# A fused attention and expert kernel: the weight maxima and weight splits of the opening in another order

## The reference, cut to what matters

```python
x = L0_attn_x                                   # (4, 1024, 512) float32
xn = _layernorm(x, axis=-1)
x = x + attn(xn, Wq, bq, Wk, bk, Wv, bv, Wo, bo) + ffn(xn, gate_w, w1, w2)

# attn: 16 heads of 32
q, k, v = proj(Wq, bq), proj(Wk, bk), proj(Wv, bv)
scores = einsum('bhqd,bhkd->bhqk', q, k) / sqrt(D)
scores = where(causal, -inf, scores) + alibi_bias
out = einsum('bhqk,bhkd->bhqd', softmax(scores), v) @ Wo.T + bo

# ffn: 8 experts, every token goes to its 2 best
probs = softmax(x @ gate_w.T); topw, sel = top_k(probs, 2); topw /= sum(topw)
out = sum over the chosen e of topw[e] * ((silu(g_e) * u_e) @ w2[e].T)   # g_e, u_e = split(x @ w1[e].T)
```

## Time and profile before

| | us |
|---|---|
| median of 3 runs | 1640.9 |
| lowest and highest | 1637.94, 1645.32 |
| the profiled execution's own time | 1637.66 |
| its span, first to last instruction | 1635.9 |
| PE busy in the span | 1479.2 (90%) |
| mean granted TensorE clock | 0.976 |

### The profile page before, as it was taken

One profiled execution on the slowest core, in us unless ns is written; L12 is line 12 of the kernel. 1 busy time (PEld: TensorE's weight loads), 2 busy tenths in 40 slices (PEclk: granted clock), 3 DMA queues, 4 the chain that ended last, 5 costly groups with the idle time before them and its releaser, 6 DMA issues.

```text
span 1635.9 us, 35508 instructions
## 1 busy us (share of the span) xinstructions
PE 1479.2 (90%) x12763; PEld 889.9 (54%) x12763; DVE 1047.6 (64%) x2485; ACT 888.6 (54%) x2029; POOL 567.1 (35%) x595
## 2 busy tenths in 40 slices
PE   3799988998998899989799898999889999999995
PEld 1465555655555555655455466565356656566563
DVE  6688787666778767777878877777334333333331
ACT  4477776665777666676766565667312222222221
POOL 3111132121113222112311134231215777777775
PEclk9899999999999999999999899999989999999998
DMA  6244431433423243542324241324687888788783
GB/s 254 74 131 114 123 91 58 112 104 101 118 90 96 88 136 115 149 128 76 97 64 116 77 115 52 87 78 164 220 260 110 136 129 141 129 140 136 127 145 45
DMA packets 171350, 193.28 MB, mean 118 GB/s; under 512 B 87536, under 2 KB 121072, under 8 KB 171056
## 3 DMA queue, kind: packets, MB, share of 16 engines
q1 hardware_dynamic: 143760, 151.67, 34.3%
q0 software_dynamic: 26128, 37.24, 13.7%
q10 hardware_dynamic: 1296, 2.11, 0.3%
HBM read 93.45 MB, written 53.74 MB: 90 GB/s over the span
## 4 chain that ended last, share of the span: by engine, by line
PE 67%; DVE 11%; issue 7%; ACT 5%; DMA 4%; SPq 4%; POOL 2%; DVEq 0%; POOLq 0%; ACTq 0%
PE S L1175 15%; PE T L1098 11%; PE O L1114 7%; PE S L1055 5%; PE S L1087 5%; PE O L1206 4%; PE M L1206 4%; PE M L1055 4%; DVE arena L1480 4%; SPq L932 3%; PE S L1072 2%; PE M L1137 2%; PE M L1072 2%; ACT arena L1670 2%; DVE arena L1491 1%
## 5 line engine op out<-in xcount | busy, mean ns | idle before, releaser
L1480 DVE CUSTOM_DVE_ANT_0 arena<-S,cF,nsl 128x1024 f32<-128x1024 f32 (+7 forms) x512 | 413.2, 811 | 60.0 <-PE S L1087 56.9
L1098 PE MATMUL T<-cF,arena 128*128 128x128 f32 x2304 | 368.1, 281 | 77.4 <-ACT arena L1684 42.6
L1670 ACT ACTIVATE arena<-arena,mneg 128x1024 f32<-128x1024 f32 (+7 forms) x512 | 395.4, 772 | 47.8 <-DVE mneg L1480 46.8
L1684 ACT ACTIVATE arena<-T 128x512 f32<-128x512 f32 (+3 forms) x544 | 241.8, 457 | 276.3 <-PE T L1098 274.2
L1098 PEld LDWEIGHTS T<-cF,arena 128*128 128x128 f32 x2304 | 267.9, 142 | 179.2 <-ACT arena L1684 47.8
L1175 PE MATMUL S<-arena 128*128 x1704 | 270.4, 316 | 8.9 <-issue 8.9
L1823 POOL DMA_INDIRECT out<-arena x142 | 222.1, 1564 | 106.8 <-ACT arena L1730 53.7
L1491 DVE COPY arena<-T 128x512 f32<-128x512 f32 (+3 forms) x288 | 153.6, 536 | 138.8 <-PE T L1098 137.0
L1175 PEld LDWEIGHTS S<-arena 128*128 128x128 f16 x1704 | 167.9, 99 | 108.4 <-issue 10.3
L1114 PE MATMUL O<-arena 128*32 128x128 f32 (+1 forms) x3328 | 211.3, 330 | 8.3 <-DVE arena L1511 7.1
L1087 PE MATMUL S<-arena 96*128 96x512 f16 (+3 forms) x768 | 213.1, 332 | 3.8 <-DMA arena<-arena 2.5
(11 more groups left out here) (187 smaller groups left out, 1822.3 us busy)
## 6 DMA issues: line engine op xcount, KB each, us to landing
arena<-arena SPq DMA_DIRECT2D x192, 128.0 KB, 2.4
arena<-in_w1T SPq DMA_DIRECT2D x64, 352.0 KB, 3.5
arena<-in_x SPq DMA_DIRECT2D x64, 256.0 KB, 3.4
w_d<-arena SPq DMA_DIRECT2D x32, 352.0 KB, 2.9
arena<-w_d SPq DMA_DIRECT2D x16, 704.0 KB, 7.2
arena<-in_w2T SPq DMA_DIRECT2D x32, 256.0 KB, 2.9
out<-arena SPq DMA_DIRECT2D x32, 256.0 KB, 3.2
xn_d<-arena SPq DMA_DIRECT2D x24, 256.0 KB, 2.0
```

What stands on the lines that cost most here:

```text
L1098: tp = pe.transpose(z[:, (c - c0) * P:(c - c0 + 1) * P], ring[u % 4][:, c * P:(c + 1) * P], idf)
L1480: dve.tensor_tensor_reduce(ring[r][:, 0:w], SBK[o.bank["score", u]][:, 0:w], rel[:, S - w:S], nsl[:, hh:hh + 1], 3.0e38, ALU.add, ALU.min, ...
L1670: act.activation(ring[r][:, 0:w], ring[r][:, 0:w], ACT.Exp, bias=mneg[:, m:m + 1], scale=-1.0, accum_out=rs[:, k, c:c + 1]).then_inc(sems[ ...
L1684: act.activation(PT[k][:, h, to_:to_ + gap * (c1 - c0 - 1) + 1:gap, :], TB[o.bank["tr", u, i]][:, 0:n].rearrange("p (c n) -> p c n", n=P), ...
```

## The change

Both halves' statistics stay first. Then the first half is normalised as before, and its transposes go to the two T banks in place of the M banks. All four `tops` now come ahead of any `xn` of the second half; the second half's four `xn` stand in pairs around the two steps of `gmax` and `gtop`. The weights' group 0 is split into q, k and v (pieces 0, 1, 2, of 512 columns each), and pieces 3 to 6 are the other groups. PE's waits follow: q of group 0 waits for `wql` 0, k for 1, v for 2, anything later for 6. `scales` 1 is cut in three: 1 (seven small instructions), 3 (`cq`, `bq`, `bk`) and 4 (the gate's, the slopes and `rel`). The second half's turns are placed around the first `qk`. k of group 0 gets a float32 place of its own, in the second half of `raw`, so a `qk32` waits for the `qkl` two before it. The float16 halves of tiles 3 to 6 move from `st` to the arena behind `PT1`, so the waits for their release move from `qkh` to the first `pt` of unit 8 and up. `otop` moves ahead of `vsb`, and `woh` and `wol` are cut into halves.

```diff
     def ln_turn(b, half, i):
...
+        bank = "M" if b else "T"
...
-    for half in range(2):
-        for i in range(7):
-            if i > 2:
-                ln_turn(0, half, i - 3)
-                flush()
-            if i < 4:
-                ln_tile(0, half, i)
-        if half == 0:
-            add("tops", 0)
+    for i in range(7):
+        if i > 2:
+            ln_turn(0, 0, i - 3)
+            flush()
+        if i < 4:
+            ln_tile(0, 0, i)
     load["act"] = load["dve"]
-    for c in range(1, 4):
+    for c in range(4):
         add("tops", c)
...
     for part in range(2):
-        for _ in widest("w", part):
-            pass
+        first = widest("w", part)
+        next(first)
+        ln_tile(0, 1, 2 * part)
+        ln_tile(0, 1, 2 * part + 1)
+        next(first)
     add("scales", 0)
     add("wqh", 0)
+    add("scales", 1)
+    add("wqh", 1)
     add("wql", 0)
-    for c in range(4):
-        add("wqh", 1 + c)
-    add("scales", 1)
+    add("wql", 1)
+    add("scales", 3)
+    for i in range(2):
+        ln_turn(0, 1, i)
+        flush()
+    add("wqh", 2)
+    add("wqh", 3)
+    add("wql", 2)
     start = qkv_steps(0, 0)
     for i in range(16):
         next(start)
         flush()
-        if i == 5:
-            add("wql", 1)
+        if i == 2:
+            for t in (2, 3):
+                ln_turn(0, 1, t)
+            flush()
+            add("wqh", 4)
+        elif i == 4:
+            add("wql", 3)
+            add("wqh", 5)
+        elif i == 8:
+            add("scales", 4)
+            add("wqh", 6)
+        elif i == 11:
+            add("wql", 4)
+    next(start)
+    add("otop")
     for _ in start:
         flush()
-    for c in range(1, 4):
-        add("wql", 1 + c)
+    add("wql", 5)
+    flush()
+    add("wql", 6)
 
     def first_rest():
-        add("otop")
-        yield
...
-        add("woh")
-        yield
-        add("wol")
+        add("woh", 0)
+        yield
+        add("wol", 0)
+        add("woh", 1)
+        yield
+        add("wol", 1)
         yield
...
-        return w[:, :, :, 0:P] if part == 0 else w[:, part - 1, :, P:E]
+        return w[:, :, part, 0:P] if part < 3 else w[:, part - 3, :, P:E]
+
+    def t32_at(b, g, qk, half):
+
+        return raw[:, 1, 0:512] if b == g == 0 and qk else t32[:, 0, :]
...
-                if (b, g, qk, half) != (0, 0, 0, 0):
-                    n = 4 * (b * NG + g) + 2 * half + qk - 1
-                    on.wait_ge(sems["qkl"], n + 1)
+                n = 4 * (b * NG + g) + 2 * half + qk
+                if n > 3:
+                    on.wait_ge(sems["qkl"], n)
+                elif n > 1:
+                    on.wait_ge(sems["qkl"], n - 1)
```

More of the change, by code:

```diff
@@ L188, in ln_turn @@
         key = "xtp", b, half, i
-        take_m(*key)
+        bank = "M" if b else "T"
+        if b:
+            take_m(*key)
+        else:
+            o.take("T", *key)
         add(*key)
@@ L195, in rest @@
             o.count["xt", b, half, i] = o.count["xt", b, half, i, en]
-            o.leave("M", key, ("xt", b, half, i))
+            o.leave(bank, key, ("xt", b, half, i))
         later.append(rest)
@@ L1129, in tensor @@
                 if third == 0:
-                    on.wait_ge(*at("wol"))
+                    on.wait_ge(*at("wol", 1))
                     for g in range(NG):
@@ L1490, in vector @@
                     on.wait_ge(*at("pv", u // 8 * 8 - 9))
+                elif u >= 8:
+                    on.wait_ge(*at("wol", 1))
+                    for t in range(3, 7):
+                        on.wait_ge(*at("xtp", 0, t // 4, t % 4))
+                        on.wait_ge(*at("xnd", 0, t // 4, t % 4))
                 dve.tensor_copy(PT[k][:, h, to_:to_ + gap * (c1_ - c0_ - 1) + 1:gap, :],
@@ L1628, in scalar @@
                 tt = half * 4 + i
-                tz = MBK[o.bank["xtp", b, half, i]][:, :].bitcast(F16)
+                tz = (MBK if b else TB)[o.bank["xtp", b, half, i]][:, :].bitcast(F16)
                 on.wait_ge(*at("xtp", b, half, i))
@@ L1680, in scalar @@
                 else:
-                    on.wait_ge(*at("wql", 4))
+                    on.wait_ge(*at("wql", 6))
                     if u >= 8:
-                        on.wait_ge(*at("wol"))
+                        on.wait_ge(*at("wol", 1))
+                        for t in range(3, 7):
+                            on.wait_ge(*at("xtp", 0, t // 4, t % 4))
+                            on.wait_ge(*at("xnd", 0, t // 4, t % 4))
                 act.activation(PT[k][:, h, to_:to_ + gap * (c1 - c0 - 1) + 1:gap, :],
```

56 lines of the change are left out of this document (30 added, 26 removed).

## The result

The changed kernel takes **1629.88 us**, median of 5 runs (1626.0 to 1632.59); the kernel before took 1640.9, median of 5 (1637.94 to 1645.32; the three runs known ahead and two more). The ratio is 0.9928 with a 95% interval of 0.9902 to 0.9954: 11.0 us less. The profiled execution is one of the faster ones: own time 1626.15, span 1624.4, PE busy 1476.2 us (91%), mean granted clock 0.974.

A forecast was written before the change was run, and what follows sets the result against it. PE was taken as the bound from about 100 us on, so the opening's saving shifts everything behind it: 10.7 at unit 2 plus 0.5 from woh is 11.2, so 11; 1640.9 - 11 = 1629.9 us, range 1625 to 1637.

The forecast's parts named there:

- The maxima and the xn: Opening on DVE: three further reductions follow the first at once in 5.06; second half's first two xn take 0.48 each.
- The chain ahead of the copy: Opening: PE's turn of tile 3, gmax, two small DVE steps and two xn, then the copy of the maxima to 25.05.
- Waits behind POOL: DVE beside POOL's second-half xnl: 0.6 of waiting for the scale and 0.6 for the first wql, bounds 0 and 1.16 each.
- Rival 1: Small DVE scale instructions wait for POOL's xnl; gain falls by 2.7 to 8.5, time 1632.4; chance 0.24.
- q's low clock: First q matmuls on PE: q takes 3.94 as before, start to start, its first matmuls at 1.2 GHz.
- The second float32 place: k of group 0's own float32 place: worth nothing by itself, since PE still has v to do.
- The first mx: End of the opening on DVE: at 52.5, behind two wql of 1.36, against 59.3; 6.8 earlier.
- otop: Its 2.28 moves to a DVE pause before v; it and PE's wait for it are gone behind the first mx.
- The halves of woh and wol: Output weights' split: about 1 us of PE's 2.68 wait can return; taken as 0.5, bounds 0 and 1.9.
- The pt assignment: Different choice of ACT or DVE for some pt between units 0 and 16: 0, bounds -0.5 and 0.5.
- Nothing of the change reaches there: From about 100 us on PE is the bound, so what the opening saves shifts everything behind it.
- Rival 3: Long part of the kernel: mean granted clock falls to 0.96, costing 24 us, time 1654; chance 0.04.

The follow-up runs named there:

- tops_late: Changed kernel with only the first reduction of the weights ahead of the second half's xn, the other three behind them; 1631.48 us, ratio to before 0.9932.
- pt_before: Changed kernel with the fifteen pt copies of units 0 to 14 that differ put back on the engines of the kernel before; 1623.39 us.
- again: The changed kernel's same code profiled once more, for a second trace; 1624.93 us.
- warm: Changed kernel plus 27 idle matmuls with overwritten results in PE's pauses of the opening; 1620.77 us, ratio to before 0.9879.
- t32_one: Changed kernel with q and k of group 0 sharing one float32 place again, as before; 1623.02 us.
- otop_late: Changed kernel with otop, the maximum of the output weights, behind the first mx again, as before; 1634.85 us.
- o_whole: Changed kernel with the high and low part of the output weights in one instruction each, as before; 1621.96 us.
- best3: Changed kernel with gwh and gwl right behind otop, before's pt copy engines, and 12 idle matmuls before the first score; 1617.07 us, ratio 0.9876.

## Why the prediction was right, and where not

The predicted time was 1629.9, the measured one 1629.88. That closeness is in part luck: errors of up to 4 us in both directions cancel, and the five runs themselves lie 6.6 us apart. The mechanism of the opening is as predicted; what became of its gain behind unit 2 is not.

**The maxima and the xn: right.** Reductions of 6.73 for four and `xn` of 0.5 each stand where the sum put them. tops_late shows 5.2 us of q's start to hang on this order.

**The chain ahead of the copy: too long.** The copy of the maxima came at 24.01 instead of 24.9. About half of that is this execution: the turn of tile 3 took 0.62 (21.88), put at 1.03 as in all rows of before, and it is that short only in after and pt_before. In the other traces of the new order it takes 1.01 to 1.04 and the copy comes at 24.2 to 24.8. The rest is the sum's: `gmax` runs into the end of the turn (again: from 22.46, where the turn ends at 22.66) and was laid behind it.

**Waits behind POOL: right in kind, sizes off both ways.** The scale's two-operand step: 0.6 assumed, about 0.2 found (0.39 against 0.16 in tops_late, where POOL had ended 1.6 us before). `wql`: 0.6 assumed, 0.75 found. Together with the chain before them: q at 28.14 instead of 29.35, and with the same steps behind it the last `qkl` ends at 45.62 (46.75) and the first score starts at 49.54 (50.7).

**Rival 1, small DVE instructions wait for POOL: false for this kernel.** Ten steps with one operand on 128x1 took 0.15 each beside `xnl` (from 24.18 on), as they do without it. What did wait is wider: the 128x4 of the earlier trace rows, and in tops_late a 3x3 step for 0.93. By the page "SBUF — State Buffer" of the Trainium skill (section "Who interferes with whom") a tensor_scalar contends with GpSimd only in a mode that uses two ports, and an instruction with two SBUF inputs contends with any GpSimd instruction that reads SBUF. The trace fits both (0.15 for the one-column steps, 0.39 for the two-operand one); in which mode the small steps ran, no row shows.

**q's low clock: right, and slightly worse.** 3.94 was put from start to start; q took 4.24 from 28.14 to the turns at 32.38, beside a granted clock of 0.56 at 28 to 32 us. In warm q takes 2.75, 1.5 less, but starts 2.3 later than again.

**The second float32 place: mis-sized.** Put at 0, with v as its cover; worth 1.3 (t32_one; 0.9 to 1.6 by the first score alone). The step "its cover is that PE still has v to do" followed PE only. The end of this stretch is set by POOL's last `qkl`. (The sum had it in its times all the same, since it laid `qk32` of the second q without a wait; what was wrong is the worth given to the edit by itself.)

**The first mx: the last wait was another.** Put at 52.5, right behind the two `wql`; found at 50.61, behind a wait of 0.60 for the score, with the `wql` done at 50.0. The sum gave PE's two turns behind q 2.06 and they took 1.06 (32.38). With q's earlier start v ended at 46.56 instead of 49.0, and `vsb` and the `wql` moved with it. That is most of the 1.7 by which unit 2 beat the forecast (12.4 us earlier, not 10.7).

**otop: right, in place and size.** Unit 2 minus the first `mx` is 2.9 (put at 2.7) against 6.6 before and 6.6 in otop_late; the two `wql` behind `vsb` take 2.7 as put.

**The halves of woh and wol: mis-sized.** Put at +0.5 (0 to 1.9); worth about 0 (o_whole, 0.1 by the marks). Three waits of 1.1 to 1.5 stand where one of 2.68 and one of 0.56 were.

**The pt assignment: mis-sized.** Put at 0, bounds 0.5; it costs 0.6, or up to 1.0, since the 0.4 more that are lost in the same stretch stand at a low clock of pt_before.

**"Nothing of the change reaches there": false.** The sum let the shift of unit 2 stand to the end. In the profiled execution 2.3 of it went between units 16 and 20 to a granted clock of 0.50 at 88 to 92 us behind a wait of 0.94 that before has as well (0.83) and gets away with. After that, the shift wanders between 7.9 and 14.2 with stretches of low clock at other places in either execution. Summed over windows of 4 us, the share of clock not granted is 42.2 us after, 38.6 before, and 28.8 (best3) to 44.4 (otop_late) in the other traces. Rival 3 has this mechanism with the wrong size: not 19 us, but some 4 us up or down from one execution to the next.
